# Graph attention on one core: the issue of the values' second copy moves from SP's queue to ACT's, with a copy moved and maxima negated in pairs

## The reference

```python
def proj(W, bias):
    y = jnp.einsum('bse,fe->bsf', x, W) + bias
    return y.reshape(b, seq_len, NUM_HEADS, HEAD_DIM).transpose(0, 2, 1, 3)
q, k, v = (proj(Wq, bq), proj(Wk, bk), proj(Wv, bv))
scores = jnp.einsum('bhqd,bhkd->bhqk', q, k) * SCALE
mask = (adj_matrix + bond_matrix)[:, None, :, :]      # both are adj
scores = scores * mask
attn = jax.nn.softmax(scores, axis=-1)
ctx = jnp.einsum('bhqk,bhkd->bhqd', attn, v)
ctx = ctx.transpose(0, 2, 1, 3).reshape(b, seq_len, EMBED_DIM)
return jnp.einsum('bse,fe->bsf', ctx, Wo) + bo
...
x = _layernorm(x + _L0_gnn_ref(...))
```

## Time and profile before

| | |
|---|---|
| median of 3 runs | 419.25 us (416.65 to 419.89) |
| the profiled execution, its own time | 418.86 us |
| its span in the profile | 416.3 us |
| PE busy | 382.1 us (92%) |
| DVE busy | 386.2 us (93%) |
| ACT busy | 361.6 us (87%) |
| POOL busy | 249.6 us (60%) |
| SP's DMA queue (q1) | 66.35 MB, 63.9% of the 16 engines |
| ACT's DMA queue (q10) | 25.17 MB, 18.0% |
| the chain that ended last | DVE 33%, PE 28%, DMA 12%, SP's queue 11%, issue 9%, ACT 4% |

### The profile page before, as it was taken

One profiled execution on the slowest core, in us unless ns is written; L12 is line 12 of the kernel. 1 busy time (PEld: TensorE's weight loads), 2 busy tenths in 40 slices (PEclk: granted clock), 3 DMA queues, 4 the chain that ended last, 5 costly groups with the idle time before them and its releaser, 6 DMA issues.

```text
span 416.3 us, 12182 instructions
## 1 busy us (share of the span) xinstructions
PE 382.1 (92%) x3628; PEld 291.4 (70%) x3628; DVE 386.2 (93%) x1592; ACT 361.6 (87%) x1223; POOL 249.6 (60%) x379
## 2 busy tenths in 40 slices
PE   8989999999996999999999999899999999997772
PEld 6766777777674877777777776677777777675542
DVE  4988999999997799999999999999999999999865
ACT  4699999989897798999999999889899999999560
POOL 3143557677573775748577575757758474555455
PEclk9999999999999899999999999999999999999898
DMA  8468889989988789889989888888999898888632
GB/s 272 131 173 238 236 201 254 245 237 247 244 237 234 191 223 244 244 243 251 253 237 246 241 237 235 230 242 233 248 245 248 227 232 208 219 234 183 144 105 76
DMA packets 65427, 92.29 MB, mean 222 GB/s; under 512 B 8529, under 2 KB 48722, under 8 KB 65362
## 3 DMA queue, kind: packets, MB, share of 16 engines
q1 hardware_dynamic: 47426, 66.35, 63.9%
q10 hardware_dynamic: 17936, 25.17, 18.0%
HBM read 26.22 MB, written 8.39 MB: 83 GB/s over the span
## 4 chain that ended last, share of the span: by engine, by line
DVE 33%; PE 28%; DMA 12%; SPq 11%; issue 9%; ACT 4%; POOL 1%; DVEq 0%; ACTq 0%; POOLq 0%
DVE boxes L540 15%; DVE probs L521 13%; SPq L208 9%; DMA v_boxed<-v 8%; PE ctx_bank L404 7%; PE out_bank L421 5%; PE proj_bank L333 5%; PE out_bank L351 4%; PE row_bank L264 3%; ACT probs L728 3%; DMA carried<-boxes 3%; PE turn_bank L281 2%; SPq L217 2%; DVE stats L567 1%; DVE low_top L530 1%
## 5 line engine op out<-in xcount | busy, mean ns | idle before, releaser
L728 ACT ACTIVATE probs<-probs,low_top 128x256 f32<-128x256 f32 x512 | 254.6, 504 | 12.1 <-DVE low_top L530 12.1
L521 DVE CUSTOM_DVE_ANT_0 probs<-row_bank,adj_rows 128x256 f32<-128x256 f32 x512 | 187.4, 414 | 6.7 <-PE row_bank L264 5.9
L540 DVE STREAM_TRANSPOSE boxes<-probs 128x1536 f32<-128x1536 f32 x62 | 109.6, 1768 | 0.0
L333 PE MATMUL proj_bank<-xt_parts,w_parts 128*128 128x512 f32 x360 | 99.2, 411 | 0.0
L728 ACT ACTIVATION_READ_ACCUMULATOR probs<-probs,low_top 128x1 f32 x512 | 99.1, 194 | 0.0
L333 PEld LDWEIGHTS proj_bank<-xt_parts,w_parts 128*128 128x128 f32 x360 | 62.9, 188 | 30.5 <-issue 19.9
L404 PE MATMUL ctx_bank<-carried,v_boxed 128*32 128x256 f32 x744 | 61.9, 392 | 18.3 <-DMA v_boxed<-v 12.2
L867 POOL COPY wide<-shares 128x512 f32<-128x512 f32 x32 | 19.5, 610 | 92.2 <-DVE shares L548 92.2
L264 PE MATMUL row_bank<-kq 32*128 32x256 f32 x1024 | 73.3, 400 | 0.5 <-DVE top L521 0.5
L404 PEld LDWEIGHTS ctx_bank<-carried,v_boxed 128*32 128x32 f32 x744 | 32.3, 111 | 43.4 <-issue 31.4
L264 PEld LDWEIGHTS row_bank<-kq 32*128 32x128 f32 x1024 | 46.3, 184 | 11.7 <-issue 6.4
(11 more groups left out here) (85 smaller groups left out, 461.1 us busy)
## 6 DMA issues: line engine op xcount, KB each, us to landing
carried<-boxes SPq DMA_DIRECT2D x248, 192.0 KB, 3.9
xt<-in_x_t SPq DMA_DIRECT2D x32, 256.0 KB, 3.5
adj_rows<-in_adj ACTq DMA_DIRECT2D x32, 256.0 KB, 4.8
xr<-in_x ACTq DMA_DIRECT2D x32, 256.0 KB, 3.8
v_boxed<-v SPq DMA_DIRECT2D x124, 64.0 KB, 3.0
out<-result ACTq DMA_DIRECT2D x31, 256.0 KB, 5.3
w_whole<-in_wk ACTq DMA_DIRECT2D x2, 128.0 KB, 3.7
w_whole<-in_wq SPq DMA_DIRECT2D x1, 256.0 KB, 4.3
```

Of the source, the lines that this page charges most:

```text
L333: last = nc.tensor.matmul(proj_bank[:], w_parts[:, a, which, t, c * P:(c + 1) * P], xt_parts[:, pair % 2, b, t, :], start=(half_ == 0 and ...
L521: last = nc.vector.tensor_tensor_reduce(probs[:, h % RING, t * S:(t + 1) * S], row_bank[j][:, t * S:(t + 1) * S], adj_rows[:, (g // 2) % 2 ...
L540: nc.vector.transpose(boxes[:, n % BOXES].rearrange("p a h (f q) -> p (h f) a q", q=D), probs[:, first:first + BOXED, :].rearrange("p h (f ...
L728: last = nc.scalar.activation(tile, tile, ACT.Exp, bias=low_top[:, g % 2, J * c + j, t:t + 1], accum_out=sums[:, g % 2, t, j * T + c:j * T ...
```

## The change

- `carry_v` moves from SP's program to ACT's. ACT issues the four DMAs of graph g+1 in step g behind the exponentials of s = 2 (in step 0: those of graph 0 behind s = 2 and those of graph 1 behind s = 6).
- `copy_v(g+1)` moves from s = 3 to s = 1, behind the exponentials and `move_turned` (step 0: stays at 5).
- `load_masks(g+2)` moves from s = 2 to s = 4 (step 0: stays at 2).
- The copies of values are counted on four semaphores in place of two.
- `lower_top` for one head becomes `lower_tops` for two: one instruction on 128x2x2 values behind head 2's reduction, one behind head 3's.

```diff
--- before.py
+++ after.py
@@ -100,9 +100,10 @@
         wk_in = [sem(f"wk_in{t}") for t in range(T)]
         weight_in = {n: sem(f"weight_in_{name}") for n, name in ((1, "q"), (2, "v"), (3, "o"))}
         biases_in = sem("biases_in")
-        stored, v_in = ([sem(f"{name}{n}") for n in range(2)] for name in ("stored", "v_in"))
-
-        x_in, adj_in, carried_in = ([sem(f"{name}{n}") for n in range(4)] for name in ("x_in", "adj_in", "carried_in"))
+        stored = [sem(f"stored{n}") for n in range(2)]
+
+        x_in, adj_in, v_in, carried_in = (
+            [sem(f"{name}{n}") for n in range(4)] for name in ("x_in", "adj_in", "v_in", "carried_in"))
 
         xt_in = [[sem(f"xt_in{n}_{t}") for t in range(T)] for n in range(2)]
         xt_first = [sem(f"xt_first{t}") for t in range(T)]
@@ -209,15 +210,6 @@
                                  boxes[D * i:D * (i + 1), n % BOXES].rearrange("p j h f -> p j (h f)")
                                  ).then_inc(carried_in[n % 4], 16)
 
-            def carry_v(n):
-
-                sp.wait_ge(v_ready, n + 1)
-                wait(sp, ctx_made, n - 3)
-                for j in range(J):
-                    sp.dma_start(v_boxed[j::J, (n // 2) % 2, n % 2].rearrange("p t e -> p (t e)"),
-                                 v[D * j:D * (j + 1), (n // 2) % 2, n % 2].rearrange("p t e -> p (t e)")
-                                 ).then_inc(v_in[n % 2], 16)
-
             for t in range(T):
                 load_x_t(1, t)
             for n, dram in ((2, wv), (3, wo)):
@@ -227,13 +219,10 @@
             for pair in (2, 3):
                 for t in range(T):
                     load_x_t(pair, t)
-            carry_v(0)
 
             def step(g):
                 if 0 < g <= LAST:
                     carry_boxes(2 * g - 1)
-                if 0 <= g + 1 < LAST:
-                    carry_v(g + 1)
                 if g > 0 and is_pair((g + 1) // 2 + 3):
                     load_x_t((g + 1) // 2 + 3, (g + 1) % 2)
                 if 0 <= g < LAST:
@@ -371,7 +360,7 @@
             def weigh_v(g):
                 pe.wait_ge(v_ready, g + 1)
                 if g < LAST:
-                    pe.wait_ge(v_in[g % 2], 64 * (g // 2 + 1))
+                    pe.wait_ge(v_in[g % 4], 64 * (g // 4 + 1))
                 if g == 0:
 
                     pe.wait_ge(bias_ready, 1)
@@ -524,11 +513,12 @@
                         top[:, g % 2, J * c + j, t:t + 1])
                 last.then_inc(rows_used, 1)
 
-            def lower_top(n, j):
-                g, place = n // T, J * (n % T) + j
-                dve.wait_ge(rows_used, J * n + j + 1)
-                nc.vector.tensor_reduce(low_top[:, g % 2, place, :], top[:, g % 2, place, :].unsqueeze(2), AXIS.X, ALU.max,
-                                        negate=True).then_inc(top_ready, 1)
+            def lower_tops(n, half_):
+
+                g, place = n // T, J * (n % T) + 2 * half_
+                dve.wait_ge(rows_used, J * n + 2 * half_ + 2)
+                nc.vector.tensor_reduce(low_top[:, g % 2, place:place + 2, :], top[:, g % 2, place:place + 2, :].unsqueeze(3),
+                                        AXIS.X, ALU.max, negate=True).then_inc(top_ready, 2)
 
             def box(n):
 
@@ -655,11 +645,11 @@
 
                 for j in range(J):
                     reduce_rows(n, j)
-                    if j > 0:
-                        lower_top(n, j - 1)
+                    if j == 2:
+                        lower_tops(n, 0)
                     if j == 1 and n % T == 0 and n > 0:
                         divide(n // T - 1)
-                lower_top(n, J - 1)
+                lower_tops(n, 1)
 
             def step(g):
                 if is_group(2 * g):
@@ -774,6 +764,15 @@
                 nc.scalar.copy(v[:, (n // 2) % 2, n % 2].rearrange("p t e -> p (t e)"),
                                out_bank[:]).then_inc(v_ready, 1)
 
+            def carry_v(n):
+
+                act.wait_ge(v_ready, n + 1)
+                wait(act, ctx_made, n - 3)
+                for j in range(J):
+                    act.dma_start(v_boxed[j::J, (n // 2) % 2, n % 2].rearrange("p t e -> p (t e)"),
+                                 v[D * j:D * (j + 1), (n // 2) % 2, n % 2].rearrange("p t e -> p (t e)")
+                                 ).then_inc(v_in[n % 4], 16)
+
             def high_last(half_):
                 act.wait_ge(last_ctx, half_ + 1)
                 if half_ == 0:
@@ -817,14 +816,18 @@
                         read_kq(1, 0)
                     if s == 1 and g == 0:
                         copy_v(0)
-                    if s == 2 and is_graph(g + 2):
+                    if s == 2 and g == 0:
+                        carry_v(0)
+                    if s == (2 if g > 0 else 6) and 0 <= g + 1 < LAST:
+                        carry_v(g + 1)
+                    if s == (4 if g > 0 else 2) and is_graph(g + 2):
                         load_masks(g + 2)
                     if s == 1 and is_group(2 * g - 1):
                         move_turned(2 * g - 1)
+                    if s == (1 if g > 0 else 5) and is_graph(g + 1):
+                        copy_v(g + 1)
                     if s == 6 and is_graph(g):
                         load_x(g)
-                    if s == (3 if g > 0 else 5) and is_graph(g + 1):
-                        copy_v(g + 1)
                     if s == (3 if g > 0 else 4) and is_pair(ahead):
                         read_kq(ahead, 2 * (g % 2) + 1)
                     if s == 3 and is_graph(g - 1):
```

## The result

The changed kernel takes 518.17 us (median of 6 runs, 514.22 to 527.9), the kernel before 416.7 in the same comparison: ratio 1.237, 95% interval 1.229 to 1.246. The profiled execution took 516.68 us, its span is 514.4. The forecast was 456, with a range of 427 to 470. The direction was right; the kernel lost some 100 us where 37 had been forecast.

A forecast was written before the change was run, and what follows sets the result against it. Bound before: a two-graph loop through PE, DVE and SP's box issues, 11.9 us a graph. Then ACT closes last: 10.59 + 1.00 + 1.65 = 13.24 a graph; 418.86 + 33.6 + 3.3 = 455.8, so 456 us, range 427 to 470.

The forecast's parts named there:

- What bounds the kernel: A two-graph loop through PE, DVE and SP's box issues, whose landing releases PE: 23.79 us, 11.9 a graph.
- The stall and its place: On ACT before exponential 3, which waits until the fourth issue has ended: 1.65 us a step (0.65 to 2.2).
- c+0.60: On ACT, c being the start of its copy of values: the first issue starts about 0.60 us later.
- the end of the running ahead: ACT's instruction stream, waiting for its copy of values, no longer leads its engine; only exponential 2, 0.99 us, is queued.
- the loop through the reciprocal: ACT and DVE between steps: 1.00 us from last exponential's end to next first exponential, where it was 0.75.
- The price of an issue: Values' issues on ACT's queue: 2.46 us for four, as on SP at 17.42 us; bounds 1.46 and 3.0.
- PE near 85%: PE's busy share in the changed kernel, listed among the signs that the forecast is right.
- its copy: ACT's copy of values, two exponentials sooner: wait for PE's values taken as 0, upper end 0.6 us.
- The pairs: DVE's masking groups: maxima negated in pairs save 0.13 us a group, 0.26 us of DVE work a graph.
- rival 2: ACT's issues run beside its engine without a stall; the two-graph loop decides: 408 to 416 us, chance 0.08.
- 1, cheap issues: Issues on ACT cost 0.334 us like its loads, stall 0.65: 425 to 430 us; chance 0.20 including prices between.
- 3, boxes landing later: Values and masks on ACT's queue delay the last box by 1.5 us at most: 435 us, chance 0.05 alone.

The follow-up runs named there:

- e8: The kernel before with the values' second copy issued by ACT, one issue behind each of exponentials 4 to 7, and four semaphores: 422.52 us, ratio 1.007.
- e1: The changed kernel with only the issue of the values' second copy (`carry_v`) back on SP: 424.35 us, ratio 1.020.
- e3: The kernel before with the four issues in a row behind exponential 4 on ACT, and the four semaphores: 447.44 us, ratio 1.073.
- e10: The changed kernel without the box issues of every second group from group 5 on: 465.94 us.
- e6: The changed kernel with only two of the four box issues of each group from group 4 on: 513.21 us, ratio 1.227.
- e7: The changed kernel with eight matmuls that serve nothing in TensorE's gap ahead of its turning: 491.89 us, ratio 1.176.
- e2: The kernel before with the maxima negated in pairs (`lower_tops`) and nothing else: 421.37 us, ratio 1.011.
- e4: The changed kernel with the four issues spread on ACT, one behind each of exponentials 2 to 5: 440.95 us.

## Why the prediction was wrong

**What bounds the kernel: held.** e8 shows that taking the four issues off SP gives nothing even where ACT doesn't stand still for them, as argued from the boxes' landing. That PE waits for the boxes, where the label said values, fits e1 as well: there the same place is labelled "DMA carried<-boxes".

**The stall and its place: held to 0.03 us.** The first issue (c+0.61 for c+0.60), the end of the running ahead, the handing over after the fourth issue, the loop through the reciprocal (1.03 for 1.00) are all in the rows. The other runs show the cover's part, that is, how much of the issues hides under work already queued on ACT: the same issues cost 91 us in the changed kernel, 30 in e3 and about 3 in e8.

**The price of an issue: the step that failed first.** The prediction said "so the price lies in the transfer's shape and not in a busy queue" and took 2.46 us for four. They took 3.8 on the mean of steps 1 to 29 (0.95 each), and the gap had a mean of 2.99 us for 1.65. The row at 17.42 us was right for what it showed, four issues with nothing of this kind in flight, and e10 gives 2.41 for ACT. The median of 0.596 was right too, for issues that stand behind the boxes in one queue. The error was to apply them to a moment at which another queue issues as well: the copy of values ends just when DVE finishes the boxes of the odd group, and in all but one of steps 2 to 29 SP's first box issue starts 0.2 us before or after ACT's first issue of values, so the two bursts always meet. ACT's and SP's third and fourth issues there, from the timelines at 331 to 333 us:

```profile
330.85 1.13 ACTq L772 DMA_DIRECT2D v_boxed<-v  x1
...
332.01 1.37 ACTq L772 DMA_DIRECT2D v_boxed<-v  x1
```

```profile
331.15 0.85 SPq L209 DMA_DIRECT2D carried<-boxes  x1
...
332.04 1.36 SPq L209 DMA_DIRECT2D carried<-boxes  x1
```

They end together, at 331.98 and 332.00, and again at 333.38 and 333.40. The prediction weighed what the Trainium skill, "Perfetto Trace Analysis", section "DMA Instruction — HWDGE (DVE, Sync)", says of a lock shared by two sequencers, and dropped it because the mask loads on ACT were not lengthened. Here too the first two issues of each burst overlap freely (0.48 and 0.61 with 0.54 and 0.61; in the 16 steps in which SP's burst starts first, ACT's second issue takes 1.3), and in e6 an issue was held for 1.20 us with nobody else issuing. So taking turns does not explain it, but that the queues are independent, which I concluded from single loads, is refuted for bursts.

What holds an issue stays open. e10 shows that without the boxes' burst beside them the issues are cheap, but it takes away the issuing and the transfers at once. Transfers in flight alone don't do it: in the kernel before, the issues of values stand right behind a box burst that is still in flight and mostly take 0.6 each. Nor are the engines simply full: in the stretch from 329.70 to 333.40 they are busy 0.66 of the time, in the box burst before (308.0 to 311.2) 0.97. That an issue waits for a place that an earlier transfer gives back, on whichever queue, fits e6 and e10 and the long packet there, but what fills up was not measured. The prediction even had a row of it: the fourth box issue of a burst takes 1.03 us where the first takes 0.54. It was read as SP's private pressure.

**The clock: not in the sum at all.** e7 prices it at 24 us, the work of the fillers included. The prediction's list named "PE near 85%" and stopped there. Stalls of 3 us on ACT become stops of 1.9 to 5.2 us on PE, ahead of its turning, and behind 16 of the 30 stops the clock falls. Such steps take up to 17.5 us for 14.4. The harm goes on for a step: PE is late with the values, ACT waits for them at its copy, by 0.76 us or more in most cases (11.4 us in all, which the prediction took as 0), and its second issue then meets the boxes too and takes 1.3 us for 0.61. Eight steps of 15.5 to 15.8 us hold no half clock themselves; each follows one that does.

**The pairs: a saving that wasn't there.** The prediction took 0.13 us less of DVE work a group. The group became 0.03 us longer (3.13 for 3.10), since the term left out the wait of the last negation, and e2 is 1.1% slower. This was in no term of the 456, only in the time of rival 2.

**The sum, mended:** the mean step of e7 is 14.48 us where 13.24 was forecast, and 29 times the difference is 36 us, of which 34 are the gap (2.81 for 1.65). 456 + 36 = 492, and e7 took 491.9; without the fillers it is 24 more, 516 for 515.5 measured. The last microsecond is luck: e7 reaches step 1 at 30.68 us, where 28.6 was forecast, and is 2 us shorter from step 30 on.

**Rivals.** 1, cheap issues, is out: even single ones take 0.48. 2, no stall, is out. 3, boxes landing later, played no part in the changed kernel, where PE's waits for boxes are 3.4 us in all. In e4 they are 29.9, and in e1 20.7, hardly more than before the change (18.3, under both labels).

## What to carry to other kernels

An engine that computes may issue DMAs only as many as fit under what is queued ahead of them: put one behind each longer instruction (which only avoided the loss here, e8), and never a row of them behind a wait for the engine's own last result. Price an issue from rows in which the same neighbours are in flight, not from one that stands alone; in a burst the later issues carry the price. When an engine is made to wait, ask which engine waits for it next and whether that one keeps its clock. And before merging small operations, look at what runs in the hole that the merged one will leave.

## What the runs showed of the hardware

Issues of this transfer (32 rows of 2 KB within on-chip memory) take 0.48 us alone on ACT's queue (e8) and 0.56 to 0.59 on SP's (the kernel before); in a row of four with nothing of SP's in flight 0.48, 0.61, 0.62, 0.61 (e10); beside a burst of box moves up to 1.6, mean 0.95. Issues of two queues in such a burst can end within 0.02 us of each other. In e10 the issues of 0.74 to 1.88 us went with a packet of 16 KB of the instruction queue on one engine. Adding eight useless matmuls a step made the kernel 24 us faster, with the mean granted clock at 0.984 in place of 0.925.
